# A transformer block in split fp32: new order of the projections between the scores, new SBUF addresses for queries, keys and feed forward

## What is computed

```
h = layernorm(x, ln1);  x = attention(h, h, sa_wq, sa_wk, sa_wv, sa_wo, sa_bo) + x
h = layernorm(x, ln2);  x = attention(h, cond_emb, ca_wq, ca_wk, ca_wv, ca_wo, ca_bo) + x
h = layernorm(x, ln3);  a, gate = split(h @ ff_w1 + ff_b1)
out = a * gelu(gate) @ ff_w2 + ff_b2 + x
attention: softmax(q @ k.T * 64 ** -0.5) @ v, heads joined, @ wo + bo
```

## Time and profile before

| what | value |
|---|---|
| median of 3 runs | 2836.69 us |
| the profiled execution's own time | 2836.61 us |
| its span, first to last instruction | 2834.8 us |
| mean granted TensorE clock | 0.999 of 2.4 GHz |
| HBM read and written | 94.52 and 49.02 MB |

### The profile page before, as it was taken

One profiled execution on the slowest core, in us unless ns is written; L12 is line 12 of the kernel. 1 busy time (PEld: TensorE's weight loads), 2 busy tenths in 40 slices (PEclk: granted clock), 3 DMA queues, 4 the chain that ended last, 5 costly groups with the idle time before them and its releaser, 6 DMA issues.

```text
span 2834.8 us, 72539 instructions
## 1 busy us (share of the span) xinstructions
PE 2809.7 (99%) x25278; PEld 2512.7 (89%) x25278; DVE 2266.4 (80%) x3495; ACT 1913.5 (67%) x6041; POOL 1461.8 (52%) x1310
## 2 busy tenths in 40 slices
PE   7999999999999999999999999999999999999999
PEld 6888888888888888888888888888888889999999
DVE  6888888888888888888989889988999855555554
ACT  6777777777777777877777777777777744444443
POOL 5444444444444444755555555555555545544554
PEclk9999999999999999999999999999999999999999
DMA  6666666666666666767777776666666632222222
GB/s 151 151 163 164 160 159 157 160 153 155 150 151 150 153 152 155 171 172 176 178 177 175 175 176 169 168 164 167 170 165 163 153 101 74 74 79 86 76 74 64
DMA packets 355329, 413.33 MB, mean 146 GB/s; under 512 B 122016, under 2 KB 209440, under 8 KB 355232
## 3 DMA queue, kind: packets, MB, share of 16 engines
q1 hardware_dynamic: 345088, 395.29, 57.2%
q10 hardware_dynamic: 10144, 16.78, 1.9%
HBM read 94.52 MB, written 49.02 MB: 51 GB/s over the span
## 4 chain that ended last, share of the span: by engine, by line
PE 94%; DVE 3%; POOL 2%; ACT 1%; issue 0%; DMA 0%; ACTq 0%; DVEq 0%; POOLq 0%
PE unit_ps L612 52%; PE unit_ps L637 15%; PE s_ps L625 14%; PE s_ps L612 13%; POOL probs L1325 1%; DVE neg_max L1075 1%; DVE blocks L1089 1%; POOL w_lo L1320 0%; DVE qk_lo L1100 0%; DVE hT_lo L1113 0%; ACT probs L884 0%; DVE hT L1070 0%; ACT x_n L861 0%; DMA x_ln<-in_x_dram 0%; DVE w_lo L1041 0%
## 5 line engine op out<-in xcount | busy, mean ns | idle before, releaser
L1325 POOL TENSOR_TENSOR probs<-probs,row_inv 128x1024 f32<-128x1024 f32 x512 | 969.7, 1894 | 1059.0 <-DVE row_inv L1080 1058.9
L884 ACT ACTIVATE probs<-s_ps,neg_max 128x256 f32<-128x256 f32 x2048 | 947.7, 484 | 407.4 <-DVE neg_max L1075 406.2
L1089 DVE STREAM_TRANSPOSE blocks<-probs 128x1024 f32<-128x1024 f32 x512 | 633.8, 1238 | 124.0 <-POOL probs L1325 121.3
L1075 DVE TENSOR_REDUCE neg_max<-s_ps 128x4 f32<-128x1024 f32 x512 | 614.1, 1200 | 13.5 <-PE s_ps L625 8.4
L612 PE MATMUL unit_ps<-hT_hi,w_hi 128*128 128x256 f32 x2048 | 566.2, 280 | 3.9 <-DVE hT_lo L1113 3.7
L612 PE MATMUL unit_ps<-hT_hi,w_lo 128*128 128x256 f32 x2048 | 553.8, 277 | 0.0
L612 PE MATMUL unit_ps<-hT_lo,w_hi 128*128 128x256 f32 x1792 | 495.8, 277 | 0.0
L637 PE MATMUL unit_ps<-pT,v_f 128*64 128x256 f32 x4096 | 456.6, 381 | 0.0
L884 ACT ACTIVATION_READ_ACCUMULATOR probs<-s_ps,neg_max 128x1 f32 x2048 | 440.4, 215 | 0.0
L612 PE MATMUL unit_ps<-w_hi,a_hi 128*128 128x256 f32 x1536 | 437.8, 285 | 2.2 <-POOL a_lo L1340 1.0
L612 PE MATMUL unit_ps<-w_lo,a_hi 128*128 128x256 f32 x1536 | 426.4, 278 | 0.0
(11 more groups left out here) (73 smaller groups left out, 6011.3 us busy)
## 6 DMA issues: line engine op xcount, KB each, us to landing
pT<-blocks SPq DMA_DIRECT2D x1024, 256.0 KB, 4.5
rows_t_dram<-row_blocks SPq DMA_DIRECT2D x91, 256.0 KB, 2.3
rows_in<-rows_t_dram SPq DMA_DIRECT2D x91, 256.0 KB, 4.9
x_res<-in_x_dram SPq DMA_DIRECT2D x32, 256.0 KB, 3.1
x_sa_dram<-x_out SPq DMA_DIRECT2D x32, 256.0 KB, 2.2
x_ln<-x_sa_dram ACTq DMA_DIRECT2D x32, 256.0 KB, 4.7
ctx_in<-in_ctx_dram SPq DMA_DIRECT2D x32, 256.0 KB, 4.1
x_res<-x_sa_dram SPq DMA_DIRECT2D x32, 256.0 KB, 3.4
```

The lines of the kernel that those rows point to most:

```text
L884: op = nc.scalar.activation(probs[:, m % 2, r, :].rearrange("p (j b c) -> p j b c", j=IT, c=BLK), scored.rearrange("p (j c b) -> p j b c", ...
L1075: nc.vector.tensor_reduce(neg_max[:, m % RING, :], s_ps[:, m % 2, :, :].rearrange("p h (i j) -> p (h i) j", j=S), AX_X, ALU.max, negate=Tr ...
L1089: nc.vector.transpose(blocks[:, n % 2, :, m % 2, :].rearrange("p b (j r c) -> p r j b c", j=IT, c=BLK), probs[:, m % 2, :, :].rearrange("p ...
L1325: nc.gpsimd.tensor_tensor(probs[:, m % 2, :, :], probs[:, m % 2, :, :], row_inv[:, m % RING, :].unsqueeze(2).broadcast_to([P, ROWS, S]), A ...
```

## The change

Gaps 0, 2 and 3 now begin with queries and keys and end with the output projection or V. Gap 3 of a steady iteration computes the queries of three pairs, then the keys of three pairs, then the whole of wo0 (for the first batches wo0 comes first). The banks are dealt out anew. `scores` waits for its own pair's remainder instead of for two. DVE makes the remainder of pair 2 right behind the first maxima.

Queries and keys lie in one tensor: keys 368 elements (1472 bytes) behind the queries, slots 2560 bytes apart, remainders 10752 bytes behind the high parts. Feed forward gets its own addresses: rows and hidden values inside `pT`, from 64 bytes on; the remainders of the first weight 128 bytes further on in `w_lo`; the second weight inside `qk`, from 320 bytes on.

First batches: the split of the second half of the V weight moves one step forward on ACT and POOL, one V product moves from gap 1 to gap 2, and a dummy exponential loads ACT's table at the start. Last batch: the feed-forward weights are split earlier, one remainder on POOL instead of DVE, a dummy gelu loads the table, the rows are turned in a scores bank before the attended units, and the third attended unit comes ahead of the output projection. Lines that only follow from renaming are left out.

```diff
@@ -28,6 +28,8 @@
+K_BEHIND_Q, QK_APART, QK_RING = 368, 640, 2688
+SHIFTED_W1, SHIFTED_W2, SHIFTED_ROWS = 32, 80, 16
@@ -51,20 +53,20 @@
-    ((("v", 0, 0), "cur"), (("qk", 6), "cur"), (("qk", 7), "cur"), (("v", 0, 1), "cur"), (("v", 1, 0), "cur"),
+    ((("qk", 6), "cur"), (("qk", 7), "cur"), (("v", 0, 0), "cur"), (("v", 0, 1), "cur"), (("v", 1, 0), "cur"),
...
-    ((("wo", 0), "prv"), (("qk", 0), "nxt"), (("qk", 1), "nxt"), (("qk", 2), "nxt")),
+    ((("qk", 0), "nxt"), (("qk", 1), "nxt"), (("qk", 2), "nxt"), (("wo", 0), "prv")),
...
-BANK_OF = {("qk", 3): 0, ("qk", 4): 3, ("qk", 5): 1, ("wo", 1): 2,
-           ("a", 0): 0, ("a", 1): 3, ("a", 2): 1, ("a", 3): 2,
-           ("v", 0, 0): 0, ("qk", 6): 3, ("qk", 7): 1, ("v", 0, 1): 0, ("v", 1, 0): 2, ("v", 1, 1): 3, ("x",): 0,
-           ("wo", 0): 1, ("qk", 0): 0, ("qk", 1): 3, ("qk", 2): 2}
+BANK_OF = {("qk", 3): 3, ("qk", 4): 2, ("qk", 5): 1, ("wo", 1): 0,
+           ("a", 0): 3, ("a", 1): 0, ("a", 2): 1, ("a", 3): 2,
+           ("qk", 6): 0, ("qk", 7): 3, ("v", 0, 0): 1, ("v", 0, 1): 2, ("v", 1, 0): 0, ("v", 1, 1): 1, ("x",): 3,
+           ("qk", 0): 3, ("qk", 1): 2, ("qk", 2): 0, ("wo", 0): 1}
...
-LAST_ATTENDED = (0, 3, 0, 3)
-TURNED = 2
+LAST_ATTENDED = (3, 2, 0, 3)
+TURNED, DOWN = 2, (1, 3)
@@ -98,7 +100,7 @@
-    early = [(("v", 0, 0), "cur"), (("v", 0, 1), "cur")]
+    early = [(("v", 0, 0), "cur")]
@@ -212,8 +214,9 @@
-qk_hi = sb("qk_hi", [P, RING, 2, S], F32R)
-qk_lo = sb("qk_lo", [P, RING, 2, S], F32R)
+qk = sb("qk", [P, 2 * QK_RING], F32R)
+qk_hi, qk_lo = ([qk[:, o + r * QK_APART:o + r * QK_APART + 2 * K_BEHIND_Q].rearrange("p (a s) -> p a s", a=2)[:, :, 0:S]
+                 for r in range(RING)] for o in (0, QK_RING))
@@ -228,8 +231,22 @@
+transposed = pT[:].rearrange("p n j u x -> p (n j u x)").bitcast(F32R)
+rows_hi_at, rows_lo_at = SHIFTED_ROWS, SHIFTED_ROWS + 2 * DK * S
+hid_hi_at = rows_lo_at + 2 * DK * S + 64
+hid_lo_at = hid_hi_at + FT * S
+ff_rows_hi = transposed[:, rows_hi_at:rows_hi_at + 2 * DK * S].rearrange("p (o k s) -> p o k s", o=2, k=DK)
+ff_rows_lo = transposed[:, rows_lo_at:rows_lo_at + 2 * DK * S].rearrange("p (o k s) -> p o k s", o=2, k=DK)
+hid_hi = transposed[:, hid_hi_at:hid_hi_at + FT * S].rearrange("p (m s) -> p m s", m=FT)
+hid_lo = transposed[:, hid_lo_at:hid_lo_at + FT * S].rearrange("p (m s) -> p m s", m=FT)
+ff_w1_lo = w_lo[:].rearrange("p s n -> p (s n)")[:, SHIFTED_W1:SHIFTED_W1 + DK * WCOLS].rearrange(
+    "p (k n) -> p k n", k=DK)
+ff_w2_hi = qk[:, SHIFTED_W2:SHIFTED_W2 + WCOLS]
+ff_w2_lo = qk[:, SHIFTED_W2 + WCOLS:SHIFTED_W2 + 2 * WCOLS]
...
+table = sb("table", [P, IT])
@@ -382,10 +399,10 @@
-    return placed(t, n, {(-1, 3): [1], (0, 0): [3]}, {})
+    return placed(t, n, {(-1, 3): [1], (0, 0): [3], (0, 1): [5]}, {})
...
-    return placed(t, n, {(-1, 1): [0], (-1, 3): [2], (0, 0): [4], (0, 1): [5], (1, 0): [6], (1, 1): [7]},
+    return placed(t, n, {(-1, 1): [0], (-1, 3): [2], (0, 0): [4], (1, 0): [6], (1, 1): [7]},
@@ -395,7 +412,7 @@
-    return placed(t, n, {(-1, 1): [0], (-1, 3): [1, 2, 3], (0, 0): [4], (0, 1): [5], (1, 0): [6], (1, 1): [7]},
+    return placed(t, n, {(-1, 1): [0], (-1, 3): [1, 2, 3], (0, 0): [4, 5], (1, 0): [6], (1, 1): [7]},
@@ -615,15 +632,14 @@
-        if m % 2 == 0:
-            pe.wait_ge(at.qk_lo, g + 2)
+        pe.wait_ge(at.qk_lo, g + 1)
...
-                    last = nc.tensor.matmul(s_ps[:, m % 2, hd, it * S:(it + 1) * S], q[part, r, 0, rows],
-                                            k[part, r, 1, :], start=n == 0, stop=n == 2)
+                    last = nc.tensor.matmul(s_ps[:, m % 2, hd, it * S:(it + 1) * S], q[r][part, 0, rows],
+                                            k[r][part, 1, :], start=n == 0, stop=n == 2)
@@ -665,6 +681,21 @@
+    def queries(b, m, home):
+        ph = pass_of(b, home)
+        if m == 0:
+            pe.wait_ge(at.x_lo, b + 1)
+        if isinstance(b, int) and b == ph.first and m % 2 == 0:
+            piece_done(pe, ph, ("qk", m))
+        product(unit_ps[:, bank_of(("qk", m)), 0:S], projection(0, slice(m * P, (m + 1) * P), 0, slice(0, S)))
...
+    def keys(b, m, home):
+        ph = pass_of(b, home)
+        if m == 0 and ph.has_ctx:
+            pe.wait_ge(at.ctx_lo, 2 * (b - ph.first + 1))
+        product(unit_ps[:, bank_of(("qk", m)), S:2 * S],
+                projection(1, slice(m * P, (m + 1) * P), ph.kv, slice(0, S))).then_inc(at.qk_full, 1)
@@ -710,40 +733,38 @@
-                           [term for k in range(DK) for term in three(w_hi[:, k, cols], w_lo[:, k, cols],
-                                                                      hT_hi[:, parity, k, :], hT_lo[:, parity, k, :])])
+                           [term for k in range(DK) for term in three(w_hi[:, k, cols], ff_w1_lo[:, k, cols],
+                                                                      ff_rows_hi[:, parity, k, :],
+                                                                      ff_rows_lo[:, parity, k, :])])
...
-        for it, bank in enumerate((unit_ps[:, 0, :], unit_ps[:, 1, :])):
+        for it, bank in enumerate(unit_ps[:, i, :] for i in DOWN):
...
-            last = product(bank[:, 0:D], three(a_hi[:, m, rows], a_lo[:, m, rows],
-                                               w_hi[:, 2, m * D:(m + 1) * D], w_lo[:, 2, m * D:(m + 1) * D]),
+            last = product(bank[:, 0:D], three(hid_hi[:, m, rows], hid_lo[:, m, rows],
+                                               ff_w2_hi[:, m * D:(m + 1) * D], ff_w2_lo[:, m * D:(m + 1) * D]),
...
-    def transpose_rows(b):
+    def transpose_rows(b, bank):
...
-                last = nc.tensor.transpose(unit_ps[:, TURNED, k * S + it * P:k * S + (it + 1) * P],
+                last = nc.tensor.transpose(bank[:, k * S + it * P:k * S + (it + 1) * P],
...
-        pe.wait_ge(at.wo_done, 2 * last)
-        transpose_rows(0)
+        pe.wait_ge(at.wo_done, 2 * last - 1)
...
-        attend(last, 2, ca)
...
-        pe.wait_ge(at.exp_done, TOTAL * PAIRS)
@@ -756,10 +777,13 @@
-        pe.wait_ge(at.v_done, 4 * t + 2)
+        pe.wait_ge(at.exp_done, TOTAL * PAIRS)
+        transpose_rows(0, s_ps[:, 1, 1, :])
+        pe.wait_ge(at.v_done, 4 * t + 4)
...
-        pe.wait_ge(at.v_done, 4 * t + 4)
...
+        pe.wait_ge(at.wo_done, 2 * t)
+        attend(t, 2, ca)
@@ -771,12 +795,15 @@
-                at.bank_free(pe, t, ("wo", 0))
-                project_out(t - 1, 0, 0, home)
-                run_unit(t, home, ("qk", 0), "nxt")
-                run_unit(t, home, ("qk", 1), "nxt")
-                run_unit(t, home, ("qk", 2), "nxt")
-                project_out(t - 1, 0, 1, home)
+                if by_tensor(t + 1):
+                    run_unit(t, home, ("wo", 0), "prv")
+                for m in range(3):
+                    at.bank_free(pe, t, ("qk", m))
+                    queries(t + 1, m, home)
+                for m in range(3):
+                    keys(t + 1, m, home)
+                if not by_tensor(t + 1):
+                    run_unit(t, home, ("wo", 0), "prv")
@@ -971,13 +995,19 @@
-            early = evacuated[:{0: 2 if parts == START else 1, 1: 1, 2: 1 if parts == START else 2, 3: 2}[n]]
+            early = evacuated[:{0: 2 if parts == START else 1, 1: 1, 2: 1, 3: 2}[n]]
+            late = evacuated[len(early):]
+            if late and late[0][0] == ("qk", 7) and late[1][0] == ("v", 0, 0):
+                late[:2] = late[1::-1]
...
+            if n == 3 and parts == LAST:
+                act.wait_ge(at.qk_full, TOTAL * PAIRS)
+                split_ff_weight(0)
@@ -989,12 +1019,11 @@
-            for user in evacuated[len(early):]:
-                if user[0] == ("v", 1, 1) and "nxt" in parts:
-                    if not in_context:
-                        split_rows(t + 1, False)
-                    if to_context:
-                        split_context(t + 1)
+            for user in late:
+                if user[0] == ("v", 1, 1) and "nxt" in parts and not in_context:
+                    split_rows(t + 1, False)
+                if user[0] == ("v", 1, 0 if in_context else 1) and to_context:
+                    split_context(t + 1)
@@ -1010,9 +1039,12 @@
+                split_ff_weight(1)
+                nc.scalar.activation(table[:], neg_half[:], ACT.Gelu)
...
-                attended_hi(t, 1)
...
+    act.wait_ge(const_ready, 1)
+    nc.scalar.activation(table[:], neg_half[:], ACT.Exp)
@@ -1160,15 +1192,13 @@
+        scale_transposed(0, s_ps[:, 1, 1, :])
...
-        split_ff_weight(0)
-        scale_transposed(0)
-        split_ff_weight(1)
...
+        attended_lo(last, 2)
...
-        attended_lo(last, 2)
@@ -1193,6 +1223,8 @@
+            if n == 0 and "prv" in parts:
+                qk_remainders(t, 2)
@@ -1206,10 +1238,10 @@
+            if n == 3 and parts == LAST:
+                split_ff_weight(0)
...
-            if n == 0 and "prv" in parts:
-                qk_remainders(t, 2)
@@ -1238,6 +1270,8 @@
```

(8 more changed lines are left out.)

53 lines of the change are left out of this document (20 added, 33 removed).

## The result

The changed kernel takes 2843.68 us (median of 10 runs, 2841.99 to 2844.71), the kernel before on the same chip 2836.72 (10 runs): ratio 1.0025, 95% interval 1.0015 to 1.0034. It is slower, where 2801 us was forecast. The profiled execution has a span of 2840.6 us against 2834.8, at the same granted clock of 0.999 of 2.4 GHz, so 5.8 us are to be found.

What follows compares the result with a forecast made beforehand. The prediction took TensorE (PE), busy 99% of the span, as the bound, with DVE at 80%. Gains of 11, 8.7, 6.3, 4, 3.3 and 3 less 1 lost made 35.3, so 2836.6 became 2801 us; range 2790 to 2808 (chance 0.52).

Runs made afterwards that it cites:

- a7_rows_early: Changed kernel with DVE's remainder of the next rows, in cross attention, moved ahead of the reciprocals that start POOL's sixth normalisation: 2825.8 us, ratio 0.9963 against the kernel before.

## What to carry to other kernels

Read the busy share of every engine by stage, and where an engine has 90% of a stage, add its waits for the others: if none of them leads back to the bottleneck, it may be a bottleneck as well, and a wait taken from PE can come back as another. Follow each wait to its source: in the kernel before DVE waits 0.49 us for ACT at 1552.39, and ACT there had waited 0.66 us for PE (POOL's wait behind it covers it). A small dose of useless work on the suspected engine shows in one run whether its place has slack; it tests that place, so put one where PE doesn't already wait. And check a step's cover in each kind of iteration, by the shortest.

## What was not expected of the hardware

- A DVE subtraction with both inputs in SBUF that starts inside a POOL instruction ends a fixed time after POOL's, 0.55 us for 128x512 and 0.28 for the context's 128x256 in a7_rows_early: 2.02, 1.40 and 2.54 us for the same 128x512 that takes 0.69 alone. Work ahead of it can be moved by 0.6 us with no effect on its end.
- The pace of a matmul of 128x128 by 256 hangs on the operands' distances in SBUF and on what ran before: 0.1133 us at best, 0.118 in whole units; feed forward takes 16.48, 16.72 or 17.07 us a batch at one clock. New distances that help the scores slow the units behind them unless the gap's order changes too.
